# Attention with experts: the softmax sums inverted by logarithm, exponential and one Newton step, and the order of a unit's matmuls changed with it

## What is computed

```python
def _gqa(x, qw, qb, kw, kb, vw, vb, ow, ob):
    q = (x @ qw + qb).reshape(B, S, N_HEADS, HEAD_DIM).transpose(0, 2, 1, 3)
    k = (x @ kw + kb).reshape(B, S, N_KV, HEAD_DIM).transpose(0, 2, 1, 3)
    v = (x @ vw + vb).reshape(B, S, N_KV, HEAD_DIM).transpose(0, 2, 1, 3)
    k = jnp.repeat(k, NUM_REP, axis=1)
    v = jnp.repeat(v, NUM_REP, axis=1)
    scores = jnp.einsum('bhqd,bhkd->bhqk', q, k) / np.sqrt(HEAD_DIM)
    attn = jax.nn.softmax(scores, axis=-1)
    out = jnp.einsum('bhqk,bhkd->bhqd', attn, v)
    return out.transpose(0, 2, 1, 3).reshape(B, S, D) @ ow + ob
```

## Time and profile before

| | us |
|---|---|
| median of 3 runs (3213.11 to 3215.99) | 3213.54 |
| the profiled execution | 3213.42 |
| its span, first to last instruction | 3211.7 |
| attention stage, about | 330 to 2200 |
| one unit in the first chunk (between its first A and that of the next unit) | 55.0 |
| the four units of chunk 3 | 62.5, 59.2, 57.4, 55.0 |

### The profile page before, as it was taken

How to read it: one execution, slowest core, us unless ns; L and a number is a source line. 1 busy time by engine, 2 the same in 40 slices (tenths; PEclk the granted TensorE clock), 3 DMA queues, 4 the chain that set the end, 5 groups by cost and what they waited for, 6 DMA issues and landing times. The chain is left out here.

```text
span 3211.7 us, 45725 instructions
## 1 busy us (share of the span) xinstructions
PE 3106.2 (97%) x16848; PEld 2007.1 (62%) x16848; DVE 2110.8 (66%) x3831; ACT 1611.1 (50%) x3271; POOL 2039.1 (63%) x921
## 2 busy tenths in 40 slices
PE   6998999999999999999999999995999999999998
PEld 5776444544544544544544545532998899899996
DVE  6887788787788788788788788752343343233355
ACT  3441566566666656656556566562443343243353
POOL 3442699899899899899899899893011111111136
PEclk8997899999999999999999999997999999999999
DMA  4665532001001012111011011002333333333366
GB/s 135 210 207 163 152 134 99 14 24 47 24 24 51 21 44 70 34 34 44 18 34 46 15 36 42 27 19 104 97 79 90 74 95 76 71 94 73 76 197 239
DMA packets 132833, 251.45 MB, mean 78 GB/s; under 512 B 30603, under 2 KB 35723, under 8 KB 130085
## 3 DMA queue, kind: packets, MB, share of 16 engines
q1 hardware_dynamic: 113744, 207.61, 20.1%
q0 software_dynamic: 17440, 40.32, 6.1%
q10 hardware_dynamic: 1461, 1.11, 0.1%
HBM read 133.06 MB, written 118.62 MB: 78 GB/s over the span
## 5 line engine op out<-in xcount | busy, mean ns | idle before, releaser
L1273 DVE TENSOR_REDUCE home_mxp<-p_ps_a 128x1 f32<-128x512 f32 x2021 | 1252.5, 678 | 267.5 <-PE p_ps_a L1488 264.7
L1185 ACT ACTIVATE p_PR<-p_ps_b 128x512 f32<-128x512 f32 x2048 | 1061.2, 605 | 647.8 <-PE p_ps_b L1502 629.3
L1047 POOL TENSOR_TENSOR p_PP<-p_PP,p_PR 128x2048 f32<-128x2048 f32 x221 | 1013.7, 4587 | 57.4 <-ACT p_PR L1185 36.4
L1488 PE MATMUL p_ps_a<-home_K,home_Q 96*128 96x512 f32 x2021 | 804.2, 428 | 9.8 <-PEq L58 4.8
L1502 PE MATMUL p_ps_b<-home_Q,home_K 98*128 98x512 f32 x2048 | 786.3, 424 | 7.0 <-ACT p_PR L1185 6.8
L1043 POOL TENSOR_TENSOR p_PP<-p_PR 128x2048 f32<-128x2048 f32 x126 | 578.5, 4591 | 78.4 <-ACT p_PR L1185 74.3
L1488 PEld LDWEIGHTS p_ps_a<-home_K,home_Q 96*128 96x128 f32 x2021 | 380.0, 192 | 332.6 <-DVE home_mxp L1273 214.1
L1502 PEld LDWEIGHTS p_ps_b<-home_Q,home_K 98*128 98x128 f32 x2048 | 383.7, 189 | 308.5 <-ACT p_PR L1185 238.9
L1870 POOL DMA_INDIRECT pairs_d<-p_YE,p_token x70 | 108.4, 1548 | 723.7 <-DVE p_YE L2167 664.7
L1512 PE MATMUL p_ps_pv<-p_PR,p_VS 128*32 128x512 f32 x4096 | 512.9, 601 | 0.0
L1988 ACT ACTIVATE p_hf<-p_ps_h 128x384 f32<-128x384 f32 (+1 forms) x256 | 111.8, 437 | 530.9 <-PE p_ps_h L85 524.4
(11 more groups left out here) (223 smaller groups left out, 3319.3 us busy)
## 6 DMA issues: line engine op xcount, KB each, us to landing
weights_w_raw<-in_L_ffn_w SPq DMA_DIRECT2D x16, 2048.0 KB, 8.9
xe_d<-p_SR SPq DMA_DIRECT2D x20, 1056.0 KB, 10.4
home_Q<-qh_d SPq DMA_DIRECT2D x64, 256.0 KB, 3.7
weights_w_raw<-pairs_d SPq DMA_DIRECT2D x16, 1024.0 KB, 7.3
first_XE<-xe_d SPq DMA_DIRECT2D x16, 792.0 KB, 4.8
pairs_d<-p_SR SPq DMA_DIRECT2D x10, 1024.0 KB, 6.1
first_XE<-xe_d SPq DMA_DIRECT2D x16, 528.0 KB, 3.7
p_X<-in_x SPq DMA_DIRECT2D x8, 1024.0 KB, 8.0
```

Of the source, the lines that this page charges most:

```text
L1047: nc.gpsimd.tensor_tensor(PP[:, buf, :, :], PP[:, buf, :, :], PR[:, tile_at(u, tile), :, :], ALU.add).then_inc(add_made, 1)
L1185: nc.scalar.activation(PR[:, tile_at(u, kt), j, :], ps_b[:, n % BK, :], ACT.Exp, scale=SCALE).then_inc(ex_made, 1)
L1273: nc.vector.reduce_max(mxp[:, a // (S // CH), a % (S // CH):a % (S // CH) + 1], ps_a[:, bank, :], AXX).then_inc(a_read, 1)
L1488: nc.tensor.matmul(ps_a[:, bank, :], QS[u % QK][0:96, j, t * P:(t + 1) * P], KS[u % KV][0:96, kb * CH:(kb + 1) * CH], start=True, stop=Tru ...
```

## The change

The four reciprocals of a unit on VectorE go (they stay in the last unit). In their place, all on 128 x 512 at once: behind step 4's exponentials ScalarE takes the logarithm of the sums, into `sq`, and then the exponential of its negative, in place, which is a first guess g of the reciprocal. At the end of step 5 VectorE multiplies sums and guess, s x g, in `ps_den` (`check_guess`). At the end of step 6 it makes (s x g - 2) x g into `sq`, which is minus the reciprocal after one Newton step (`refine`). At the end of step 8 `attend` multiplies `pvs` by -1 and by `sq`, into `ps_den`. One table for logarithm and exponential is loaded on ScalarE ahead of the stage. In group 2 the logarithm also waits until the letter N has read `sq`. The strings of `BASE` are new, with as many of each letter in a unit; in `EXTRA` the second O of group 0 moves from step 13 to 12, the R of group 1 from steps 10 to 13 to 10, 11, 13 and 14, and K from step 8 to 7.

```diff
-    BASE = ["ABBABABV", "BABABB", "AAVVVABABABBAA", "BBAADABAB",
-            "ABABBABAA", "BBABAVVABA", "BABBAB", "ABVBBABA",
-            "VBABABB", "AABAVVVBABAB", "ABABBADABA", "AVABABAABB",
-            "BBAABBA", "AVAABABBAB", "BBABABAMVDVDVA", "ABABBABADA"]
-    EXTRA = {0: {11: "O", 13: "O", 15: "O"}, 1: {1: "O", 10: "R", 11: "R", 12: "R", 13: "R"}, 2: {0: "L", 1: "N", 8: "K"}, 3: {}}
+    BASE = ["BAABBABV", "BAABBABA", "VVVABABABB", "ABAABADABABA",
+            "BABABBA", "ABBABAVVABA", "BABBAB", "ABVBBAB",
+            "ABAVBBAB", "AABBAVVVABAB", "ABABABDAAB", "ABAVABABAB",
+            "ABBABAB", "ABVABABABA", "ABBABABVVMDDA", "BAABBABVADA"]
+    EXTRA = {0: {11: "O", 12: "O", 15: "O"}, 1: {1: "O", 10: "R", 11: "R", 13: "R", 14: "R"}, 2: {0: "L", 1: "N", 7: "K"}, 3: {}}
...
-    INVERT_AT, ATT_AT, LOW_AT = {4: (0,), 5: (1,), 6: (2,), 7: (3,)}, 8, 9
+    LN_AT, GUESS_AT, CHECK_AT, REFINE_AT, ATT_AT, LOW_AT = 4, 4, 5, 6, 8, 9
...
         def _(act):
             ow_raw = PR[:, PK - 1, :, :]
+            nc.scalar.preload_act_table_set("natural_log_exp_and_others")
...
+            def logarithm(u, read_to):
+
+                act.wait_ge(den_mm, NS * (u + 1))
+                if read_to:
+                    act.wait_ge(a_mm, read_to)
+                nc.scalar.activation(sq[:], ps_den[:], ACT.Ln).then_inc(inverted, 1)
+
+            def guess(u):
+
+                act.wait_ge(inverted, TT * u + 1)
+                nc.scalar.activation(sq[:], sq[:], ACT.Exp, scale=-1.0).then_inc(inverted, 1)
...
+            def check_guess(u):
+
+                dve.wait_ge(inverted, TT * u + 2)
+                nc.vector.tensor_tensor(ps_den[:], ps_den[:], sq[:], ALU.mult).then_inc(inverted, 1)
+
+            def refine(u):
+
+                dve.wait_ge(inverted, TT * u + 3)
+                nc.vector.scalar_tensor_tensor(sq[:], ps_den[:], 2.0, sq[:], ALU.subtract, ALU.mult).then_inc(inverted, 1)
+
             def attend(u):
 
                 dve.wait_ge(inverted, TT * u + TT)
                 dve.wait_ge(pvs_made, u + 1)
-                nc.vector.tensor_tensor(ps_den[:], pvs[:], ps_den[:], ALU.mult).then_inc(att_made, 1)
+                nc.vector.scalar_tensor_tensor(ps_den[:], pvs[:], -1.0, sq[:], ALU.mult, ALU.mult).then_inc(att_made, 1)
...
-                            for part in INVERT_AT.get(kt, ()):
-                                invert(u - 1, part)
+                            if kt == CHECK_AT:
+                                check_guess(u - 1)
+                            if kt == REFINE_AT:
+                                refine(u - 1)
```

More of the change, by code:

```diff
@@ L1238, in body @@
                                 projected.append(slot_of(c, g, kt, pos)[0] + 1)
-                        if kt == ATT_AT and not (first and g == 0):
-                            high(unit(c, g) - 1, (g - 1) % KV)
+                        if not (first and g == 0):
+                            if kt == LN_AT:
+                                logarithm(unit(c, g) - 1, last_slot(c, "N") if g == 2 and not first else 0)
+                            if kt == GUESS_AT:
+                                guess(unit(c, g) - 1)
+                            if kt == ATT_AT:
+                                high(unit(c, g) - 1, (g - 1) % KV)
                         if (g, kt) in SQUARES_AT and not first:
```

## The result

The changed kernel is slower. Its median is 3261.8 us in five runs (3256.7 to 3286.2), against 3216.0 us of the kernel before beside it; the ratio is 1.0153, with a 95% interval from 1.0136 to 1.0169. The forecast was 3203 us with a range from 3172 to 3232, so both the sign and the range missed. The profiled execution took 3257.3 us with a span of 3255.6 us, 43.9 us more than the span of before.

A forecast was written before the change was run, and what follows sets the result against it. TensorE's in-order stream, with VectorE and ScalarE emptying its banks, was taken as the bound. Placing, relief and attend's wait summed to -9.8 us in seven chunks and -0.6 in the first: 3213.5 - 10.4 = 3203 us, range 3172 to 3232.

The forecast's parts named there:

- What bounds the kernel: Attention stage: TensorE's in-order stream sets the pace, with VectorE and ScalarE emptying its banks; 3.6 us of waits per unit.
- So GpSimd keeps up: Attention stage: GpSimd does not set the pace; ScalarE waited for it only 8.7 us in the whole run.
- VectorE's relief: Steps 4 to 8: VectorE has 2.3 us less to do, of which a unit gains 0.4 us, between 0 and 1.0.
- ScalarE's two passes: Between step 4's and step 5's exponentials: 1.2 us hidden under TensorE's work, cost 0, up to 0.4 us if late.
- The new placing: Steps 11 to 14 without four B in a row: gain 1.2 us, price 0.5 us, so -0.7 us a unit.
- M's earlier place: Unit's end: M comes earlier relative to its V and D; no wait of TensorE for the maxima expected, 0.
- The gain of a usual unit: Later chunks: groups 1 to 3 were to gain -0.5 to -0.7 us from the order; group 0 gains 0.4, pays 0.5.
- The wait that is new: Attend, step 8, both inputs in SBUF: waits out GpSimd's running addition, 0 to 4.6 us; mean loss 0.4 us a unit.
- The hiding place behind attend: Step 9's five A and B and three V hide attend's wait up to about 1.5 us; at 2.5 us, 0.9 lost.
- The passes on ow_lo: First unit: passes splitting the output weights, 1.20 and 2.65 us beside additions against 0.68, cited as evidence for attend's wait.
- The slower case: Steps 9 and 10: attend's wait decides, +0.7 us in 31 units, +22 us, 3235 us; chance 0.25.

The follow-up runs named there:

- e3: The kernel before with only the new block order (BASE and EXTRA); reciprocals and attend as before: ratio 1.0039.
- e4: The changed kernel with the block order of before, and refine written to PSUM so that attend has one SBUF input: ratio 0.9994.
- e10: Changed kernel, attend with one SBUF input, ow_lo passes on GpSimd, new order only in first chunk and groups 2, 3; sends moved to groups 0, 1: 1.0059.
- e12: e10 with four of the sends moved to the end of group 0 and behind group 1's first addition, where GpSimd waits: 3199.8 us, 0.9943.
- e7: The changed kernel with one more wait on GpSimd, between an addition in group 1 and the pair of passes behind it: 3237.6 us, 1.0053.
- e1: The changed kernel with refine written to PSUM, so that attend reads one input from SBUF and one from PSUM: 3229.9 us, 1.0021.
- e5: e1 with the four passes on ow_lo moved from VectorE to GpSimd, ahead of its first addition: 3211.6 us, 0.9987.
- e9: The kernel before with ow_lo passes on GpSimd and the new order only in the first chunk and in group 2 of the others: 3208.4 us, 0.9966.
- e2: The changed kernel with the block order of the kernel before; new reciprocal and attend with two SBUF inputs stay: 3250.8 us, 1.0128.
- e6: The kernel before with its reciprocals written to SBUF, so that attend has two SBUF inputs: 3292.0 us, 1.0224.
- e11: The kernel before with only the four passes on ow_lo moved from VectorE to GpSimd, ahead of its first addition: 3212.2 us, 0.9981.

## Why the prediction was wrong, step by step

**What bounds the kernel**, TensorE's stream with VectorE and ScalarE emptying its banks, is not contradicted by any run. "So GpSimd keeps up" holds except in group 3, where its sends leave no room for an earlier D in step 15.

**VectorE's relief** was put at 0.4 us per unit (0 to 1.0) and is 0.02. The reason given then, that most of it lies beside V matmuls in which VectorE catches up anyway, may cover all of it; no run tests that.

**ScalarE's two passes** were put at 0, and this held: 0.63 us each. The waits for ScalarE ahead of B, seen as idle time of the weight loads, fell from 238.9 to 170.1 us in the whole run, as the order without four B in a row was to bring: e3, with that order alone, has 164.3, and e4, without it, 238.3.

**The new placing** was put at -0.7 us in a usual unit; e3 has -0.62, with 3.84 and 3.82 us in the two runs of A and B that were to take 3.6. M's earlier place was put at 0, but in e3 the weight loads wait for VectorE's maxima ahead of M (7.0 us in the kernel before) and for its split of the maxima behind M (none before). Who for whom, us in total, times, longest:

```profile
PEld p_ps_a L1488 <- DVEq L1287: 26.3, 31, 1.1
...
PEld p_ps_a L1495 <- DVE home_mxp L1273: 25.1, 30, 0.8
```

The gain of a usual unit was then carried over to the later chunks, and this step failed. Groups 0 to 3 were to change by +0.1, -0.5, -0.7 and -0.7, and changed by +0.25, +0.72, -0.47 and +0.29 in e3. That is 2.6 us a chunk, some 18 us over seven chunks between forecast and fact. For group 3 the cause is shown (e10, e12): the D of step 15 waits for an addition that the sends hold back. For group 1 it was not tested. Measured against group 2 in chunk 3 of e3, 1.1 of its 1.2 us arise in steps 11 to 15, where three of its four R stand; its old order had O and R between the B already, so that there may have been little to gain against the price of the added runs.

**The wait that is new** is the step that decided. Its mechanism was named, with its rows, and its price for a short wait was about right: a usual unit's attend of 3.06 us, 2.4 us over its own time, cost 0.80 us where 0.9 was put at 2.5. What failed is the sentence "The wait would be the rest of the addition, between 0 and 4.6 us". The wait can outlast the addition: where GpSimd's instructions follow one another without a gap, it reached 8.0 us in two places of seven. The hiding place behind attend (five A and B, three V) is then used up, TensorE stands, and its clock falls; neither was in the sum. Two such units cost 20 us in the profiled run, and e7, in which none is left, is 24 us under the changed kernel's median. The Trainium skill ("SBUF — State Buffer", section "SBUF: two separate sides") says that the loser blocks for the whole instruction of the other. The waits of 2.4 us agree; the 8.69 and 5.74 us go past one instruction.

**The passes on ow_lo** were used as evidence and not as a cost. The diff does not touch them, but the new order's first steps move them against the first addition by 1.1 us (the second pass starts 0.23 us after it instead of 0.86 ahead), and 10 us of the 43.9 lie there. In e3's profiled run, in the same order, that pass started 0.05 us ahead of the addition, took 0.68 us, and the unit took 57.6 us instead of 69.1: it is a matter of a few tenths, and the two groups of e1 suggest that it falls one way or the other from run to run. The prediction's own rows were the warning.

**The rivals.** The slower case, that the wait of attend decides, is what happened, and it had 0.25. Its price, 3235 us, came from ordinary waits in all units, which cost only some 6 to 7 us in fact (0.8 us in three units, 0.6 in group 2 of the later chunks: 57.33 us against 56.78 in e1, and nothing in the other groups). It left out the long waits, the clock and the first unit, and these carried the time past the range.

**The misses added up.** Forecast (-10.4 us) and profiled execution (+43.9) lie 54.3 us apart. An estimate from the figures above: the placing 18 us, VectorE's relief 12 (0.38 in 31 units), the wait 12 (14.6 forecast, some 26 in fact), the passes on ow_lo 10, the stage's start 3.5, less 2.1 that the forecast had held back. e5, in which attend has one SBUF input and the passes on ow_lo are not on VectorE, shows the rest of the change at 0.9987, inside the range. So the lock made the kernel slower, and the placing and the relief are why next to nothing is gained without it.

Two things stay open. The stage's start is at 331 to 336 us in the profiled runs of all these kernels, although the code ahead of it differs only by the table load on ScalarE and, in some, by the passes moved to GpSimd. The load does not explain it (e10 has it and starts at 331, e9 has not and starts at 335), so the 3.5 us there are not the change's as far as these runs show. And how many long attends the slower runs of the changed kernel have (up to 3286 us) is not seen, since one execution is profiled.

## What to carry to other kernels

When an edit makes a VectorE instruction read both inputs from SBUF while GpSimd works on SBUF too, keep one operand in PSUM: here that one choice was worth 42 to 74 us and cost no instruction. Look for passes of this kind that the edit leaves alone but moves, since a shift of some tenths of a microsecond decided whether they met an addition. And when an engine that keeps up has slack at only some places of the loop, put added work there: the same sends cost 4.8 us a unit in e10 and nothing in e12.

## What the runs showed of the hardware

- A VectorE pass with two SBUF inputs that meets a GpSimd addition ends some 0.56 us after that addition's end if GpSimd leaves a gap behind it. A gap of 0.08 us was enough in seven cases of seven (e7). Without one it lost in six of 21 (the kernel after, e2 and e6; 8.65 to 8.79 us) and won in 15; in the win shown, GpSimd's next pair of passes took 0.46 us longer.
- A send on GpSimd with an addition close behind it kept the pass out when the pass began 0.33 us or more into the send (5.58 to 5.81 us in e2 and e6), and not at 0.30 us or less (0.69 us).
- After 5.84 us without work TensorE ran at 0.50 of its clock for about 8 us, with score blocks 0.43 us apart instead of 0.23.
- The four splitting passes take 1.27 us each on GpSimd, against 0.68 on VectorE. There they run while GpSimd waits for its first addition, and moving them took some 6 us off the kernel before (e11) and 18 off e1's median (e5).
